# Prologue and attention of a two-branch attention block as one program, with a new order of the first slot

## The reference

```python
q_mid = rmsnorm(h @ q_a_w.T, q_a_ln_w)                    # 192 latents
q = (q_mid @ q_b_w.T) -> 16 heads x (128 nope + 64 rope)
kv_a = h @ kv_a_w.T                                       # 64 latents + 16 x 64 rope keys
kv = rmsnorm(kv_a[..., :64], kv_a_ln_w) @ kv_b_w.T        # 16 heads x (128 k_nope + 128 v)
scores = (q_nope k_nope + rope(q_pe) rope(k_pe)) * 192**-0.5
main_out = concat_heads(softmax(scores) @ v) @ o_w.T
# second branch, the "pattern": 16 heads of 16
pq, pk, pv = split_heads(h @ sp_q_w.T), (h @ sp_k_w.T), (h @ sp_v_w.T)
pattern_out = concat_heads(softmax(pq pk * 0.25) @ pv) @ sp_o_w.T
gates = softmax(h @ gate_w.T + gate_b)
out = gates[0] * main_out + gates[1] * pattern_out
```

## Time and profile before

| | |
|---|---|
| median of three runs | 823.15 us |
| profiled execution | 825.97 us, span 824.2 us, mean granted clock 0.976 |
| TensorE matmuls | busy 769.4 us, 93% |
| VectorE | 582.1 us, 71% |
| GpSimd | 430.2 us, 52% |
| ScalarE | 390.2 us, 47% |
| DMA | 68.13 MB, mean 83 GB/s |

### The profile page before, as it was taken

How to read it: one execution, slowest core, us unless ns; L and a number is a source line. 1 busy time by engine, 2 the same in 40 slices (tenths; PEclk the granted TensorE clock), 3 DMA queues, 4 the chain that set the end, 5 groups by cost and what they waited for, 6 DMA issues and landing times. The chain is left out here.

```text
span 824.2 us, 13732 instructions
## 1 busy us (share of the span) xinstructions
PE 769.4 (93%) x5408; PEld 479.5 (58%) x5408; DVE 582.1 (71%) x673; ACT 390.2 (47%) x489; POOL 430.2 (52%) x259
## 2 busy tenths in 40 slices
PE   6959889999899999999999999999999999989984
PEld 5734555655555556555655656565656554448763
DVE  5826655666577867866676679777857799983856
ACT  4513334555454555554545554555555454531361
POOL 1325008752865295739563955594477545460233
PEclk9979999999999999999999999999999999999988
DMA  9676453005310531082117201730353313212001
GB/s 252 250 208 214 115 143 64 14 15 130 57 35 12 119 68 49 15 141 78 41 40 142 65 2 42 124 82 2 72 91 92 108 41 116 84 46 84 1 1 51
DMA packets 97796, 68.13 MB, mean 83 GB/s; under 512 B 66434, under 2 KB 76228, under 8 KB 97476
## 3 DMA queue, kind: packets, MB, share of 16 engines
q1 hardware_dynamic: 97732, 67.25, 32.5%
HBM read 41.23 MB, written 17.04 MB: 71 GB/s over the span
## 5 line engine op out<-in xcount | busy, mean ns | idle before, releaser
L1005 POOL TENSOR_TENSOR acc<-acc,em 128x1024 f32<-128x1024 f32 x96 | 237.4, 2473 | 55.0 <-ACT em L1061 52.2
L1144 DVE TENSOR_REDUCE m2p<-xb 128x2 f32<-128x1024 f32 x128 | 156.1, 1222 | 80.5 <-PE xb L1303 80.5
L1152 DVE TENSOR_REDUCE m<-xb 128x2 f32<-128x1024 f32 x128 | 155.5, 1218 | 53.5 <-PE xb L1303 53.4
L1052 ACT ACTIVATE ep<-xb 128x1024 f32<-128x1024 f32 x128 | 131.3, 1026 | 117.6 <-PE xb L1303 117.6
L1061 ACT ACTIVATE em<-xb 128x1024 f32<-128x1024 f32 x128 | 131.2, 1025 | 93.7 <-PE xb L1303 84.4
L1339 PE MATMUL pvm<-em,cpair 128*32 128x512 f32 x1024 | 137.8, 610 | 0.0
L968 POOL TENSOR_TENSOR rot<-rot,sin 128x512 f32<-128x512 f32 x32 | 41.1, 1285 | 141.0 <-DMA rot<-raw 141.0
L1303 PEld LDWEIGHTS xb<-pq,pk 49*128 49x128 f32 x256 | 23.9, 184 | 106.8 <-issue 98.5
L1005 POOL TENSOR_TENSOR acc<-em 128x1024 f32<-128x1024 f32 x16 | 38.2, 2384 | 76.1 <-PE xb L1438 67.1
L1303 PE MATMUL xb<-pk,pq 48*128 48x512 f32 x256 | 57.0, 441 | 10.4 <-ACT ep L1052 5.6
L1350 PE MATMUL pvp<-ep,vp 128*32 128x512 f32 x512 | 66.6, 592 | 0.0
(11 more groups left out here) (272 smaller groups left out, 1300.7 us busy)
## 6 DMA issues: line engine op xcount, KB each, us to landing
rot<-raw SPq DMA_DIRECT2D x128, 64.0 KB, 2.5
pk<-spqk_d SPq DMA_DIRECT2D x48, 128.0 KB, 4.2
sums<-rec_d SPq DMA_DIRECT2D x32, 128.0 KB, 2.9
ctx_d<-ctxr SPq DMA_DIRECT2D x14, 256.0 KB, 2.1
pq<-spqk_d SPq DMA_DIRECT2D x48, 64.0 KB, 2.3
wraw<-wst_d SPq DMA_DIRECT2D x7, 384.0 KB, 6.2
em<-in_o_w SPq DMA_DIRECT2D x1, 2048.0 KB, 7.6
vp<-vp_d SPq DMA_DIRECT2D x8, 256.0 KB, 4.7
```

Of the source, the lines that this page charges most:

```text
L1005: pool.tensor_tensor(acc[:, :, :], before, em[:, j:j + 2, :], ALU.add).then_inc(added, 1)
L1052: act.activation(ep[:, j:j + 2, :], src[:, :, :], ACT.Exp, scale=PAT_SCALE).then_inc(ep_ready, 1)
L1144: dve.tensor_reduce(m2p[:, 2 * tp:2 * tp + 2, t, kt], src[:, :, :], AX, ALU.max).then_inc(x_dve, 1)
L1152: dve.tensor_reduce(m2[:, q, :, t, kt], src[:, :, :], AX, ALU.max).then_inc(x_dve, 1)
```

## The change

- `prologue` and `attention` no longer have a block each. Each returns five functions, and one block runs them one after the other on each engine. The barrier between them and SyncE's closing waits go; where attention reads what the prologue wrote, or reuses its memory, it waits on the prologue's semaphores. The order of memory allocation changes with this, and the combined weights are two tiles, `wall0` and `wall1`.
- The second store of weights (`wall1`, four pairs, 4 x 6 x 128 x 128 floats) is issued in `first_slot` behind `o_w` and `wv`.
- The transposes' evacuation `pe0T 1` moves from VectorE to ScalarE. ScalarE makes one more copy for each half, the high part of the last 64 latents into rows 64 to 127 of a new tile `qm1u`.
- The list `FIRST` has a new order; P1 comes at step 7 instead of 6, `mm 0` at step 7 instead of 12. In `first_slot` the stores of `sk 2` and `sk 3` come ahead of the rotations of P3 and P1, and `main_rows` ahead of `pattern_rows`.
- In P0 and P1 of every pair, the low weights of the last 64 latents are no longer two full passes. They are two matmuls of 64 rows, the rope part on rows 0 to 63 and the latent part on rows 64 to 127, issued one after the other at the start of the tile. The product of low weights and low latents is left out.

```diff
@@ prologue
-                ("spT", 2), ("pe1T", 0), ("lat1", 0), ("pe1T", 1), ("lat1", 1)]
+                ("spT", 2), ("pe1T", 0), ("lat1", 0), ("pe0T", 1), ("pe1T", 1), ("lat1", 1)]
...
+        def store_weights(sp, q):
+            first = int(q == 0)
+            evacuated(sp, index[("lat1", q)])
+            sp.dma_start(d["wst"].rearrange("n p c -> p n c")[:, 4 * q + first:4 * q + 4, :],
+                         wall[q][:, first:, :, :].rearrange("p n c j -> p n (c j)")).then_inc(w_stored, 16)
...
-            sp.wait_ge(s_const, 32)
-            sp.wait_ge(sp_stored, 96)
-            sp.wait_ge(w_stored, 32)
...
+                    if job[0] == "qm1T":
+                        act.activation(g["qm1u"][64:P, half_of(job[1])], bank[n % 8][64:P, :], ACT.Copy)
                     act.activation(hi_of(job), bank[n % 8][:, :], ACT.Copy).then_inc(hi_ready, 1)
@@ FIRST
-    [("P", 2)],
-    [("sk", 0), ("pm", 0), ("sv", 0)],
-    [("pm", 1), ("sk", 1), ("pm", 2)],
-    [("P", 3), ("pm", 3), ("sv", 1)],
-    [("pm", 4), ("sk", 2), ("pm", 5)],
-    [("P", 1), ("pm", 6), ("oT", 0)],
-    [("pm", 7), ("sk", 3), ("pm", 8)],
-    [("oT", 1), ("pm", 9), ("sv", 2)],
-    [("pm", 10), ("oT", 2), ("pm", 11), ("sk", 4)],
-    [("pm", 12), ("oT", 3), ("pm", 13), ("sv", 3)],
-    [("pm", 14), ("oT", 4), ("oT", 5), ("pm", 15)],
-    [("oT", 6), ("oT", 7), ("mm", 0), ("oT", 8)],
-    [("mm", 1), ("mm", 2), ("vo", 0), ("mm", 3)],
-    [("mm", 4), ("vo", 1), ("mm", 5), ("mm", 6)],
-    [("mm", 7), ("vo", 2), ("vo", 3), ("mm", 8)],
+    [("P", 2), ("sk", 0)],
+    [("sk", 1), ("pm", 0), ("sv", 0), ("pm", 1), ("pm", 2), ("sk", 2)],
+    [("pm", 3), ("sv", 1), ("pm", 4)],
+    [("pm", 5), ("P", 3), ("pm", 6), ("sv", 2)],
+    [("pm", 7), ("oT", 0), ("pm", 8)],
+    [("pm", 9), ("sk", 3), ("pm", 10)],
+    [("P", 1), ("mm", 0), ("sk", 4)],
+    [("oT", 1), ("mm", 1), ("mm", 2)],
+    [("mm", 3), ("sv", 3), ("pm", 11)],
+    [("oT", 2), ("pm", 12), ("oT", 3), ("mm", 4)],
+    [("oT", 4), ("mm", 5), ("oT", 5)],
+    [("pm", 13), ("oT", 6), ("mm", 6), ("oT", 7)],
+    [("mm", 7), ("oT", 8), ("pm", 14)],
+    [("pm", 15), ("vo", 0), ("vo", 1)],
+    [("mm", 8), ("vo", 2), ("vo", 3)],
@@ first_slot
+                sp.wait_ge(done["sp_stored"], 96)
+                sp.wait_ge(done["pe_job"], done["index"][("pe1T", 1)] + 1)
                 load_stacks(0)
                 turn(0, ORDER[0])
                 turn(0, ORDER[1])
+                sp.wait_ge(done["w_stored"], 16)
+                sp.wait_ge(done["w0_lo"], 1)
                 sp.dma_start(o_nat, ...)
+                sp.wait_ge(done["pe_job"], done["last"] + 1)
                 sp.dma_start(wv, ...)
+                done["store_weights"](sp, 1)
                 for m in range(2):
                     sp.dma_start(spo_nat[m], ...)
                 load_minus_one(0)
                 load_weights(1)
-                store_pattern(0)
-                store_pattern(1)
+                for i in range(3):
+                    store_pattern(i)
                 turn(0, ORDER[2])
-                store_pattern(2)
+                store_pattern(3)
                 turn(0, ORDER[3])
-                store_pattern(3)
                 store_pattern(4)
...
+                main_rows(0, 0)
+                pattern_rows(0)
@@ TensorE, tile P with i < 2
-                        for part in range(2):
-                            o = 2 * part
-                            mm = passes(out[:, part, :], [(hi[o], qm0h), (lo[o], qm0h), (hi[o], qm0l),
-                                                          (hi[o + 1], qm1), (lo[o + 1], qm1)])
+                        qm1u = g["qm1u"][:, half]
+                        for part, upper in enumerate((qm1, qm1u)):
+                            at = slice(64 * part, 64 * part + 64)
+                            pe.matmul(out[:, part, :], lo[2 * part + 1][at, :], upper[at, :], start=True, stop=False)
+                        for part in range(2):
+                            o = 2 * part
+                            pairs = [(hi[o], qm0h), (lo[o], qm0h), (hi[o], qm0l), (hi[o + 1], qm1)]
+                            for n, (w, x) in enumerate(pairs):
+                                mm = pe.matmul(out[:, part, :], w, x, start=False, stop=(n == 3))
```

More of the change, by code:

```diff
@@ L122, in prologue @@
         w0_hi = sem("w0_hi")
+        w0_lo = sem("w0_lo")
         w_stored = sem("w_stored")
@@ L425, in _ @@
                     dve.wait_ge(w0_hi, 1)
-                    link(dve.tensor_tensor(wst[:, 0, 6:12, :].rearrange("p c j -> p (c j)"),
-                                           wall[:, 0, :, :].rearrange("p c j -> p (c j)"),
-                                           wst[:, 0, 0:6, :].rearrange("p c j -> p (c j)").bitcast(F32), ALU.subtract))
+                    dve.tensor_tensor(wst[:, 0, 6:12, :].rearrange("p c j -> p (c j)"),
+                                      wall[0][:, 0, :, :].rearrange("p c j -> p (c j)"),
+                                      wst[:, 0, 0:6, :].rearrange("p c j -> p (c j)").bitcast(F32),
+                                      ALU.subtract).then_inc(w0_lo, 1)
+        done = {"evacuated": evacuated, "index": index, "last": len(jobs) - 1, "w0_lo": w0_lo, "xh_ready": xh_ready,
+                "xl_ready": xl_ready, "w_stored": w_stored, "sp_stored": sp_stored, "s_const": s_const, "pe_job": pe_job,
+                "store_weights": store_weights}
+        return (sync_program, pool_program, tensor_program, scalar_program, vector_program), done
 def pattern_weights(g):
@@ L513, in x_steps, with attention @@
     return steps
-def attention(nc, a, d, g):
+def attention(nc, a, d, g, sem, done):
     NS = 16
@@ L952, in _, with pool_program @@
                 sp.wait_ge(s, 64)
-        @block.gpsimd
-        def _(pool):
+        def pool_program(pool):
+            pool.wait_ge(done["pe_job"], done["last"] + 1)
+            done["evacuated"](pool, done["last"])
+            pool.wait_ge(done["s_const"], 32)
             pool.memset(vp[:, :, :, :, PD:32], 1.0).then_inc(cleared, 1)
@@ L1040, in x_tile @@
                 elif kind == "sk":
+                    if i == 0:
+                        act.wait_ge(done["sp_stored"], 96)
                     if i == 4:
@@ L1121, in produce @@
                 dve.wait_ge(raw_ready, n + 1)
+                if n == 0:
+                    dve.wait_ge(done["s_const"], 32)
                 if u < 2:
@@ L1359, in x_tile @@
                     x_emptied(pe, *x_tiles[n - NX])
+                else:
+                    done["evacuated"](pe, done["last"] - 6 + 2 * n)
                 if kind == "T":
@@ L1851, in build @@
             g |= two_types({"qm0h": [P, S], "qm0l": [P, S], "qm1": [P, S]})
+            g["qm1u"] = sbi("qm1u", [P, S], F32R)
             g |= {
@@ L1860, in build, with sem @@
             g |= {"ctx67": g["work_f"], "wst": sbi("wst", [P, 2, NW, P], F32R)}
-            prologue(nc, a, d, g)
+            phase = inner.enter_context(ExitStack())
+            def sem(name):
+                return phase.enter_context(nc.semaphore(name))
+            before, done = prologue(nc, a, d, g, sem)
             g |= {
@@ L1865, in build, with _ @@
             }
-            attention(nc, a, d, g)
+            after = attention(nc, a, d, g, sem, done)
+            block = phase.enter_context(nc.Block())
+            @block.sync
+            def _(sp):
+                before[0](sp)
+                after[0](sp)
+            @block.gpsimd
+            def _(pool):
+                before[1](pool)
+                after[1](pool)
+            @block.tensor
+            def _(pe):
+                before[2](pe)
+                after[2](pe)
+            @block.scalar
+            def _(act):
+                before[3](act)
+                after[3](act)
+            @block.vector
+            def _(dve):
+                before[4](dve)
+                after[4](dve)
+            phase.close()
             epilogue(nc, a, d, g, out)
```

90 lines of the change are left out of this document (43 added, 47 removed).

## The result

The changed kernel takes 809.6 us (median of 4 runs, 808.8 to 810.45) against 823.53 us for the kernel before beside it (4 runs, 821.94 to 824.8): a ratio of 0.9837 [0.9817, 0.9858], 13.9 us less. The forecast was 807.4. The profiled execution took 808.8 us with a span of 807.0, where the one of before had 824.2. The same kernel run once more among the experiments gave 807.14 us against 822.93, a ratio of 0.9804 [0.9781, 0.9826]. Two executions of the kernel before, beside the last experiment, were in a slower state (952.8 and 2675.4 us) and are in no median here.

What follows compares the result with a forecast made beforehand. TensorE bounds the pair slots; slot 0 also loses idle time and half clock. T0 10.7, slot 1 2.0 and query tiles 3.0 make 15.7 us: 823.15 - 15.7 = 807.4 us, 8 in 10 within 799 to 814.

Steps and rivals of the forecast that it cites:

- Part 1: Seam between prologue and attention: one program lets P0 start at about 39.7 instead of 46.82, 7.1 us; no stack wait.
- Part 2: Slot 0 in the new order: 49.0 us of TensorE work plus waits; T0 of slot 1 at 92.7 without queue trouble.
- bank waits: Slot 0, between mm 2 and pm 15: TensorE waits where VectorE tiles and oT alternate, about 2.4 us.
- half clock: Slot 0, after the idle time ahead of mm 0: TensorE runs at the lower clock, costing 1.7 us.
- Part 3: SyncE's queue in slot 0: P3's rotation reaches GpSimd at 68.7, mm 0 starts at 72.0, late by 4.4 us.
- the postponed store is paid in full by the rotation: SyncE's queue, ring order: the second weight store delays P3's rotation fully; without it the 4.4 us would be near nothing.
- the trace agrees: Claim that rows showing sp_o_w held and the rotation landing after earlier stores support the ring-order rule; no separate size.
- Slot 1: Start of slot 1: M0's wait and half clock free 3.7 us, of which 2.0 are taken as gained; bounds 0 and 3.7.
- Part 4: Query tiles P0 and P1: side-by-side low weights save one 0.23 us pass per tile, 13 tiles, 3.0 us.
- the change of mode moves into the P tile and isn't added: Query tiles: the tiling change adds nothing; were it added, each tile would lose 0.32 and gain 0.23 us.
- rival C: Query tiles: the 64-row pair costs its own drain, 0.09 us lost per tile instead of 0.23 gained; 812; chance 0.05.
- Rival A: SyncE's queue: transfers are in time, mm 0 isn't held, T0 at 92.7; 21.8 us gained, 801.3; chance 0.27.

Runs made afterwards that it cites:

- full_passes: The changed kernel with ten full passes per query tile (P0 and P1) put back: 809.22 us, ratio 0.9828 to the kernel before.
- store_early: The changed kernel with the second weight store right behind the stack loads, SyncE waiting for both stores before o_w: 810.37 us, ratio 0.9837 to the kernel before.
- spo_first: The changed kernel with sp_o_w issued ahead of o_w: 811.72 us, ratio 0.9859 to the kernel before.
- again: The changed kernel itself, run once more beside the experiments: 807.14 us, ratio 0.9804 to the kernel before.
- new_order_alone: The kernel before, two programs and barrier kept, with the new tile order, queue order and query tiles: 813.54 us, ratio 0.989 to the kernel before.
- old_order: The changed kernel with slot 0's tile order and SyncE's queue order of before: 812.42 us, ratio 0.9876 to the kernel before.
- turn_early: The changed kernel with P3's rotation issued right behind sp_o_w: 804.63 us, ratio 0.9773 to the kernel before.
- all_ahead: The changed kernel with the second store behind the stack loads (own semaphore), sp_o_w ahead of o_w, P3's rotation behind kv_b_w: 803.25 us, ratio 0.9764 to the kernel before.
- both_ahead: The changed kernel with sp_o_w, then P3's rotation, both issued ahead of o_w: 816.3 us, ratio 0.9912 to the kernel before.

## Why the prediction was right, and where its steps were off

**Part 1.** P0 was put at 39.7 and came at 39.91; the first pm tile had no wait, as taken. Whether the ScalarE copies cost anything can't be seen beside a start that differs between executions by up to 1.7 us (last transposes from 37.91 to 39.59). The merge is worth 6.7 or 8.2 us by the experiments, 7.1 by the prediction.

**Part 2 and the clock, term by term.** From P0 to T0 the prediction had 49.0 us of work, 2.4 bank waits, 4.4 for the queue, 1.6 for mrow and 1.7 of half clock, 59.1 in all. The trace has 48.6 (50.26 busy less 1.7), 0.8, then 0.84 ahead of mm 8, 3.74 (2.15 + 1.59), 1.35 and 1.7: 57.0. The mis-sized term of this sum is the bank waits: where a tile for VectorE and an oT alternate, TensorE waited 0.16 to 0.19 us four times, 0.7 in all instead of 2.4, since an mm tile with its oT takes 1.38 us by starts (81.18 to 82.56), above VectorE's 1.22, and only pm with oT is below it. What I hadn't foreseen is the weight split ahead of pm 15's maximum. T0 came at 96.88 instead of 98.8. Along the chain it reads differently. mm 0 came as forecast (below), and T0 25.02 us behind it, where the prediction had 25.1 and then 1.7 of half clock. The half clock had come earlier, ahead of mm 0 and under its wait for the rotation, where it cost T0 nothing. This is the step that put T0 1.9 us too late. Where the clock did fall behind mm 0, T0 came 26.64 us after it (full_passes), 26.36 (store_early) and 27.49 (spo_first), against 25.0 in the other two traces with this order in which mm 0 waited and the clock stayed full (again, new_order_alone).

**Part 3.** GpSimd was put at 68.7 and came at 68.45, mm 0 at 72.0 and came at 71.86. These numbers are right, and the reason given for them is so only in part. (The terms listed for the time at which mm 0 is wanted add up to 67.3, not 67.6.) The step "the postponed store is paid in full by the rotation" failed: without the store the rotation comes 1.3 to 2.4 us earlier, not 4.4 (store_early, old_order, new_order_alone), while moving the rotation itself, with the store still ahead of it, removed the whole wait (turn_early). The sentence "the trace agrees" was too much: the rows showed a rotation landing late behind stores, which any cause upstream of it would show. What sets it in this kernel is when SyncE issues it: a DMA behind kv_b_w is held 6.4 us whatever it is, and behind it about 8 us of issues for loads and pattern stores (56.00 to 64.32) follow one another before the rotation's turn; GpSimd follows the issue by 3.9 to 5.3 us in every trace. What holds an issue isn't shown. o_w and kv_b_w stood ahead of it each time, so it may be their bytes that it waits for; no run changed these. The estimate came out since I took an old interval with the same hold in it (16.74 us from o_w to GpSimd) and stretched it by bytes to 21.0 us; it was 19.99, with 2.2 us for the weight store and 1.1 for the stores of sk 2, and o_w was issued at 48.46 instead of 47.7. That the sum met the mark within 0.3 us is partly luck. The half clock came where oT 0 had waited, ahead of mm 0 (0.58 at 63.9 to 67.7), and none followed mm 0; its size was as taken, its place was not.

**Slot 1.** 3.6 us gained instead of 2.0. M0's wait and its half clock went in full: T0 to P0 took 6.21 us before (109.47 to 115.68) and 2.49 now. The drop of clock that I feared behind T0's own wait of 1.35 didn't come, and the loads behind the vo stores cost 1.25 and 1.59 us in two waits against 1.74 in the earlier trace rows. The 1.74 was followed by half clock in the kernel before (0.64 from 131.66 to 135.00), the 1.59 was not (1.00 from 116.61 to 120.00), which the prediction had not counted.

**Part 4.** 3.0 us expected; measured 2.4 [0.9, 3.8] alone and about 2.1 with the rest, neither of which excludes 3.0. The starts say it more sharply: 0.22 us at each P0, nothing at P1. In slots 1 to 7 that is 7 x 0.22 = 1.5 us, half of the forecast. From its own start to the next tile P0 now takes 2.36 us and P1 2.47 to 2.50, where 2.26 was forecast and 2.5 was named as a sign of being wrong. The step that failed is "the change of mode moves into the P tile and isn't added". For P0 it is true. P1 begins behind a wait of 0.41 us for a bank. My reading is that the wait had hidden the change, so that there it is added; the wait is in the trace of before too, and I hadn't read it. From the timeline of the kernel before:
```profile
226.13 0.73 PE L1295 MATMUL xb<-qm0h,wst 128*128 128x512 f32 x2 [0.41 <-ACT em L1061]
```
So rival C holds at half of the tiles, with about 0.2 us each instead of its 0.32. The rule of the Trainium skill ("TensorEngine Tiling (Array Packing)", "Key Properties") that a change of tiling mode drains TensorE agrees with these rows, at 0.1 us behind busy work and 0.2 us behind the wait; the rows don't show whether the time is a drain or something else at the change, such as the load of the next weights.

**The sum.** 15.7 us were forecast. The two profiles differ by 17.2, the medians by 13.9 in one comparison and 15.8 in the other, so the forecast is right within what a comparison can tell. In place of the forecast's sum, T0 gave 12.6 instead of 10.7, slot 1 3.6 instead of 2.0, and the tiles about 1.5 instead of 3.0; the rest is scatter: 1.4 us behind the pair slots are lost again where the change has no step but the last tiles, less than one program differs from itself in the stretch ahead (2.2). So misses of both signs met in the total (1.9 and 1.6 us too little, 1.5 too much), and that it is so near is partly luck. Rival A was the other likely case. Its condition was not what I named (the engines' rate) but the order of issues, and all_ahead reaches it.

## What to carry to other kernels

When a load lands late, look first at when its issue had its turn and what its queue was held by, and only then at bytes: here moving one load past the issues of nine DMAs removed its wait of 1.8 us, and 1.57 MB in its way cost it 1.3 to 2.4 us. Removing one wait of a group that share a queue needs the others listed too (ScalarE's for the store was under oT 0's), and a wait put ahead of a load in a common queue can cost more than the waits that it was to remove (both_ahead). A cost that a short wait hides comes back when work is put between the two: half of the shortened tiles gained nothing, by this reading for that reason.

## What the runs showed of the hardware

The DMA that SyncE issued behind o_w and the value half of kv_b_w (512 KB in runs of 256 bytes) was held for 6.34 to 6.50 us in the ten traces in which sp_o_w wasn't right ahead of o_w, whether it was a weight store or sp_o_w, and 7.44 us in spo_first; the weight store took 0.37 or 0.38 us elsewhere in the queue. The three kernels from all_ahead on don't show the hold: the rotation stands in its place, and it waited over 7 us for its raw tile.

How long TensorE may idle before its clock falls has no single answer in these traces. The windows behind such a wait, in the changed kernel behind the 1.59 us ahead of mm 0:
```profile
71.86:75.00 3.14, 3.14 (x12) 1.72 (x13) 2.42 (x3) 1.20 (x3) 1.26 (x1) 1.00 0.11 26
```
in all_ahead behind the 1.45 us at slot 1's stack loads:
```profile
104.62:108.00 3.38, 3.38 (x20) 2.81 (x20) 1.23 (x1) 0.57 (x1) 0.13 (x1) 0.72 1.07 322
```
and in new_order_alone behind the 2.00 us ahead of mm 0:
```profile
78.40:82.00 3.60, 3.60 (x16) 2.18 (x16) 2.59 (x4) 1.67 (x4) 1.25 (x1) 1.00 0.23 56
```
The clock stays full behind 1.59 and even 2.00 us (and behind T0's wait of 1.33 to 1.35 us in all eleven traces that have it), and falls behind 1.45 us. Behind the wait of oT 0 it fell after 2.15 us and 1.95 (again) and stayed after 1.97 (turn_early, 1.00 over the next 3.3 us). Behind M0's wait of 1.97 or 1.98 us it fell in all three traces that have it (0.50 to 0.54 over the next 3.2 us), and in old_order it fell behind 1.27 us (0.64 from 72.69 to 76.00). Behind 3.04 us and more at mm 0 it always fell (0.50 to 0.57 in three kernels). So between 1.3 and 2.2 us the length of the wait alone doesn't tell whether the clock falls, and the runs don't show what else does. It is worth up to 1.7 us a time, and my sum should have carried it as a range.

An unchanged program moved by 2.2 us in 392 us of pair slots, at a mean clock of 1.00 both times, and by up to 1.7 us in when its prologue ended.
